# A graph network on one core: statistics of the first norm by row tile, convolution tiles from the eighth count step, attention in steps of five, and ScalarE empties what VectorE emptied

## The reference, cut to what matters

```
h  = relu(layernorm(x))
xn = batchnorm(h)                                   # needs mean and variance over all 1250 rows
conv = relu(segment_mean(xn[src], dst) @ W_conv + b_conv)
q, k, v = h[:256] @ Wq, h[:256] @ Wk, h[:256] @ Wv  # 8 heads of 64
qf = exp(q@proj.T - diag - max)/16 + eps ; kf likewise  # 256 random features
att = (qf @ (kf.T v)) / (qf @ sum(kf)) @ Wo
x  = x + batchnorm(conv + att + h)
h  = relu(layernorm(x)); agg = segment_sum(h[src], dst)
x  = x + h + relu(bn(relu(bn(((1+eps)*h + agg) @ W1 + b1)) @ W2 + b2))   # as in the reference
```

## Time and profile before

| what | us |
|---|---|
| median of three runs | 421.27 |
| the profiled execution, as timed | 421.14 |
| its span, first to last instruction | 419.3 |
| TensorE busy | 384.6 (92%) |
| VectorE busy | 231.5 (55%) |
| ScalarE busy | 166.9 (40%) |
| last first-layer block (A32) handed to VectorE | 232.68 from the span's start |

### The profile page before, as it was taken

How to read it: one execution, slowest core, us unless ns; L and a number is a source line. 1 busy time by engine, 2 the same in 40 slices (tenths; PEclk the granted TensorE clock), 3 DMA queues, 4 the chain that set the end, 5 groups by cost and what they waited for, 6 DMA issues and landing times.

```text
span 419.3 us, 5944 instructions
## 1 busy us (share of the span) xinstructions
PE 384.6 (92%) x1987; PEld 279.5 (67%) x1987; DVE 231.5 (55%) x587; ACT 166.9 (40%) x292; POOL 94.2 (22%) x149
## 2 busy tenths in 40 slices
PE   2799998599869988999999998899999999999995
PEld 1587655366435644666655565545899999999992
DVE  5882889864533455572767788841235344441323
ACT  1465337275463545201002576731264445332131
POOL 7030000200000000000002268882146564011100
PEclk9999999799989999999999999999999999999998
DMA  7930203000000000000490002020000003001212
GB/s 201 274 103 4 98 3 100 2 1 2 0 2 0 3 0 2 2 2 0 122 225 2 1 2 100 29 76 2 0 2 2 2 0 100 2 11 51 61 50 73
DMA packets 16577, 17.96 MB, mean 43 GB/s; under 512 B 1813, under 2 KB 10965, under 8 KB 16537
## 3 DMA queue, kind: packets, MB, share of 16 engines
q1 hardware_dynamic: 15779, 17.28, 14.9%
q10 hardware_dynamic: 758, 0.16, 0.2%
HBM read 14.88 MB, written 2.56 MB: 42 GB/s over the span
## 4 chain that ended last, share of the span: by engine, by line
PE 64%; DVE 14%; issue 9%; ACT 7%; POOL 3%; DVEq 2%; DMA 0%; SPq 0%; POOLq 0%; ACTq 0%
PE bank L1162 62%; DVE ring L831 3%; DVE st_f L904 1%; ACT hn L610 1%; DVE hl L1050 1%; POOL ln_s L427 1%; PE bank L1183 1%; DVE w_lo L1069 1%; POOL x L465 1%; DVEq L831 1%; ACT qf L582 1%; DVE st_row L1061 1%; PE bank L1514 1%; DVE x L1058 1%; DVEq L937 1%
## 5 line engine op out<-in xcount | busy, mean ns | idle before, releaser
L1162 PE MATMUL bank<-AT,hh 125*128 125x400 f16 (+1 forms) x240 | 80.9, 339 | 2.6 <-DVE hl L1050 2.6
L1162 PE MATMUL bank<-AT,hl 125*128 125x400 f16 (+1 forms) x240 | 80.7, 338 | 0.0
L831 DVE TENSOR_SCALAR ring<-iota_code,code 125x500 f16<-125x500 f16 x200 | 54.0, 345 | 0.0
L436 POOL TENSOR_TENSOR bn_tmp<-var_eps,minus_half 128x1 f32<-128x1 f32 (+1 forms) x15 | 9.6, 642 | 189.3 <-DVE var_eps L910 189.2
L826 DVE TENSOR_TENSOR S<-iota_lane,slo 125x1024 f16<-125x1024 f16 x25 | 18.7, 750 | 57.0 <-PE bank L1162 52.3
L1162 PE MATMUL bank<-ring,S 125*128 125x500 f16 x200 | 48.5, 386 | 0.0
L1162 PE MATMUL bank<-wB,hn 128*125 128x512 f32 x80 | 38.4, 625 | 5.6 <-ACT hl L520 5.5
L1162 PEld LDWEIGHTS bank<-ring,S 125*128 125x128 f16 x200 | 28.5, 145 | 19.0 <-issue 8.3
L1162 PEld LDWEIGHTS bank<-AT,hh 125*128 125x128 f16 x240 | 23.2, 97 | 21.6 <-DVE hl L1050 3.3
L1162 PEld LDWEIGHTS bank<-AT,hl 125*128 125x128 f16 x240 | 23.3, 97 | 18.3 <-issue 0.2
L1162 PE MATMUL bank<-a_hi,w_hi 128*128 128x400 f32 (+1 forms) x96 | 34.2, 356 | 0.0
(11 more groups left out here) (190 smaller groups left out, 677.3 us busy)
## 6 DMA issues: line engine op xcount, KB each, us to landing
x_in<-x SPq DMA_DIRECT2D x5, 448.0 KB
x<-x SPq DMA_DIRECT2D x2, 1120.0 KB
w_s<-w SPq DMA_DIRECT2D x2, 1024.0 KB, 9.6
w_s<-w SPq DMA_DIRECT2D x4, 512.0 KB, 3.8
out<-x SPq DMA_DIRECT2D x8, 224.0 KB
wB<-wk SPq DMA_DIRECT2D x1, 1024.0 KB, 8.3
wA<-wq SPq DMA_DIRECT2D x1, 1024.0 KB, 12.6
wB<-wv SPq DMA_DIRECT2D x1, 1024.0 KB, 5.1
```

The lines of the kernel that those rows point to most:

```text
L436: own.step(pool.tensor_tensor(bn_tmp[:, 1, k:k + n], var_eps[:, k:k + n], minus_half[:, 0:n], ALU.pow))
L831: ins = dve.tensor_scalar(ring[:, slot, j, :], iota_code[0:CH], code[:, bass.ds(c + j, 1)], float(-CODES * t), ALU.subtract, ALU.is_equal)
L1162: return pe.matmul(o, l, r, start=start, stop=stop, skip_group_check=True)
```

## The change

The pieces move to other steps. The counts, the products and the transposes are the same instructions in the same number.

1. W_conv gets its own place (`wC`) and is loaded behind the tiles of x at the start, and not into `wB` after V1. Its sum of squares is taken by ScalarE in step 2 (`SQ_AT`), `FR` moves to step 4 and into bank 7.
2. The first norm's statistics are taken per row tile: 40 `bn_stats` of 125 columns, four for each tile in the VectorE step after the tile's transposes; the end of them is in step 5.
3. G0 moves from step 12 to step 8. V1 moves from step 7 to step 6. The attention's pieces of one head pair now repeat every five steps.
4. ScalarE's order in a step: pieces that wait for VectorE (`UQ`, `MX`) come last among the pieces; `hn` of tile i+2 comes after the AT copy of the step, and not before it.
5. `D0`, `D1` and the seven A blocks inside the steps are copied out of PSUM by ScalarE (`rdb`, and `raw` with two buffers), and VectorE works on the copies. Their statistics are taken after WO1, together.
6. `SPAN` becomes one more product in `P`. `O0` moves to bank 6; A00 to A30, A01 and A21 are in bank 7.
7. The load of x for the residual waits for WO1 alone.

```diff
 SLOTS = [s.split() for s in (
-    "hT0 hT1 hT2 K0 K1", "hT3 hT4 PT Q0", "hT5 hT6 N1 Q1", "hT7 hT8 N0 UK0", "hT9 P UQ0", "V0", "MX0", "V1 QT0",
-    "KV0 UK1 SPAN", "SQ UQ1", "FR O0 MX1", "QT1 H", "KV1 UK2 G0", "R0 O1 UQ2 G1", "R1 G2", "R2 MX2 QT2 G3",
...
+    "hT0 hT1 hT2 K0 K1", "hT3 hT4 PT Q0", "hT5 hT6 N1 Q1", "hT7 hT8 N0 UK0", "hT9 FR P UQ0", "V0", "MX0 V1", "QT0",
+    "KV0 UK1 G0", "R0 O0 UQ1 G1", "R1 G2", "R2 MX1 G3", "R3 QT1 G4", "R4 KV1 UK2 G5", "R5 O1 UQ2 G6", "R6 G7",
+    "R7 MX2 G8", "R8 QT2 G9", "R9 KV2 UK3 D0", "O2 UQ3 A00", "A10", "MX3 A20", "QT3 A30", "KV3 D1 A01",
+    "O3 A11", "TA0 TA1 A21 WO0 WO1")]
+SQ_AT, H_AT = 2, 7
...
-LAST = "A01 A11 A21 A31 D2 A02 A12 A22 A32".split()
+LAST = "A31 D2 A02 A12 A22 A32".split()
...
             def conv_high(i):
                 ps = read_group(act, f"G{i}")
                 copy(hh[:, i, :], ps[0:L, :]).then_inc(sem("s_gh"), 1)
-                if i + 2 < T:
-                    normed(i + 2)
...
+            def counts_out(name):
+                c = int(name[-1])
+                c0, w = COLS[c]
+                ps = read_group(act, name)
+                if name[0] == "D":
+                    free_group(copy(rdb[:, c0:c0 + w], ps[:, 0:w]), name)
+                else:
+                    n = RAW.index(name)
+                    if n >= 2:
+                        act.wait_ge(sem("s_raw"), n - 1)
+                    free_group(copy(raw[:, n % 2, 0:w], ps[:, 0:w]), name)
...
             for t in range(len(SLOTS)):
-                for name in SLOTS[t] if t else ():
+                for name in sorted(SLOTS[t], key=lambda name: name[:2] in ("UQ", "MX")) if t else ():
...
                 if t < NW:
                     act.wait_ge(sem("s_win"), t + 1)
                     copy(AT[:, :, t * W:(t + 1) * W],
                          banks[t % 2][0:L, 0:CODES].rearrange("p (a b) -> p a b", a=T)).then_inc(sem("s_at"), 1)
+                if t == H_AT:
+                    normed(0)
+                    normed(1)
+                for name in SLOTS[t]:
+                    if name[0] == "G" and int(name[1]) + 2 < T:
+                        normed(int(name[1]) + 2)
...
+            def tile_stats(i):
+                dve.wait_ge(free[PLACE[f"hT{i}"][0]], PLACE[f"hT{i}"][1] + 1)
+                for f in range(FB):
+                    own.mark(dve.bn_stats(st_1[:, f, i, :], hT[:, f, i * L:(i + 1) * L]))
```

More of the change, by code:

```diff
@@ L83 @@
 LONE_BANKS = {name: bank for bank, names in enumerate((
[L84 to L87, removed]
+    "", "", "K0 N1 D1 TA0", "K1 A11 TA1", "PT Q1 WO0", "Q0 N0 WO1",
+    "hT0 hT2 hT4 hT6 hT8 P MX0 MX1 MX2 MX3 KV0 KV1 KV2 KV3 O0 O1 O2 O3",
+    "hT1 hT3 hT5 hT7 hT9 FR V0 V1 D0 A00 A10 A20 A30 A01 A21 " + " ".join(f"G{i}" for i in range(T))))
+    for name in names.split()}
+LAST_BANKS = (6, 0, 1, 2, 3, 7)
 assert len(LAST_BANKS) == len(LAST)
@@ L137 @@
 W1_AT = (3, 7)
+RAW = [name for slot in SLOTS for name in slot if name[0] == "A"]
 OUT_TILES = [(0, 4), (4, 8), (8, 10)]
@@ L193, in gnn_kernel @@
         cgb = place("cgb", [P, 2, FB], F32, 7.90625)
-        sqr = place("sqr", [P, FB, D], F32, 92)
+        sqr = place("sqr", [P, FB, D], F32, 100)
         head_sel = place("head_sel", [P, FB, HEADS], F32, 7.75)
@@ L268, in gnn_kernel @@
         hn = place("hn", [P, 2, FB, L], F32, 88)
+        wC = place("wC", [P, FB, D], F32, 92)
+        raw = place("raw", [P, 2, COLS[0][1]], F32, 100)
+        st_1 = place("st_1", [P, FB, T, 6], F32, 108)
         tmpr = place("tmpr", [P, 2, COLS[0][1]], F32, 109.1875)
@@ L657, in _ @@
                         rows(i)
+                if t == SQ_AT:
+                    conv_weights()
                 if t < NW:
@@ L883, in attention @@
                     c0, w = COLS[int(name[1])]
-                    ps = read_group(dve, name)
                     dve.wait_ge(sem("s_bn1"), 1)
-                    own.step(dve.tensor_scalar(rdb[:, c0:c0 + w], ps[:, 0:w], 1.0, wscale[:, 0:1], ALU.max, ALU.mult))
-                    n_deg[0] = own.mark(dve.reciprocal(rdb[:, c0:c0 + w], rdb[:, c0:c0 + w]))
-                    dve.sem_inc(free[PLACE[name][0]], 1)
+                    d = rdb[:, c0:c0 + w]
+                    if name in LAST:
+                        ps = read_group(dve, name)[:, 0:w]
+                    else:
+                        dve.wait_ge(free[PLACE[name][0]], PLACE[name][1] + 1)
+                        ps = d
+                    own.step(dve.tensor_scalar(d, ps, 1.0, wscale[:, 0:1], ALU.max, ALU.mult))
+                    n_deg[0] = own.mark(dve.reciprocal(d, d))
+                    if name in LAST:
+                        dve.sem_inc(free[PLACE[name][0]], 1)
                 elif name[:2] == "WO":
@@ L958, in further_chunks @@
                 dve.end_ifs()
-            units = [0]
+            units, held, att_in = [0], [], [False]
             def mean_rows(name):
@@ L989, in piece @@
                 if name == "WO1":
+                    att_in[0] = True
                     own.after(own.n)
-                    for f in range(FB):
-                        own.mark(feature_stats(f, 0, hT[:, f, 0:COLS[0][1]]))
+                    for early in RAW:
+                        f, ci = int(early[1]), int(early[2])
+                        if early in held:
+                            own.mark(feature_stats(f, ci, hT[:, f, COLS[ci][0]:sum(COLS[ci])]))
             load_range(0)
@@ L1011, in _ @@
                         row_stats(i)
[L1012 to L1026, removed]
+                for name in SLOTS[t - 1] if t else ():
+                    if name[:2] == "hT":
+                        tile_stats(int(name[2]))
+                        if name == f"hT{T - 1}":
+                            own.after(own.n)
+                            for f in range(FB):
+                                own.mark(dve.bn_aggr(mv_f[:, f, :], st_1[:, f].rearrange("p c s -> p (c s)")))
+                            own.after(own.n)
+                            feature_terms(0, FB).then_inc(sem("s_mv1"), 1)
                 for name in SLOTS[t]:
@@ L1218, in attention @@
             def attention(name):
[L1219 to L1224, removed]
                 if name == "FR":
```

50 lines of the change are left out of this document (25 added, 25 removed), and 2 rows, old and new, of the table SLOTS.

## The result

The changed kernel took 429.94 us as the median of its runs (428.41 to 433.42), the kernel before 421.28 us beside it (421.06 to 421.43): a ratio of 1.0218 with an interval of 1.0156 to 1.0279. It is slower, as forecast, but by 8.7 us and not by the 2.5 of the sum, and its time lies above the range. The profiled execution took 429.83 us with a span of 428.0.

A forecast was written before the change was run, and what follows sets the result against it. TensorE was taken as the bound, losing 20.4 us to waits and slow clock; new losses 3.55 + 16.55 + 2.6 + 0.2 = 22.9 gave +2.5 on 421.14, 423.6 us; range 421.0 to 426.2, with rivals 419.0 to 427.2.

The forecast's parts named there:

- What bounds the kernel, and what is removed: TensorE's waits for ScalarE and the slow clock cost the kernel before 20.4 us between 60 and 163 us.
- The convolution term: Steps 10, 11, 12, 15, 16, 17: TensorE waits for the late hl copy, 16.55 us in all, bounds 11.5 to 18.5.
- Statistics and the early steps: Steps 4 to 8: FR, KV0 and G0 start late, 3.55 us in all; a tile's statistic costs 0.20.
- The clock: Behind three waits of over 3 us ahead of G: one and a half falls, 2.6 us; none 0, all 5.1.
- VectorE is late: Rival, chance 0.12: early tile statistics at 0.28 each add 1.6 us at KV0; with three clock falls, 427.7 us.
- the order pays: Rival, chance 0.24: clock stays at 1.00 behind all waits, KV0 and G0 wait for nothing; 17.6 us lost, 418.4 us.
- Tail, evictions, loads: No waits from step 18; the last blocks lose 0.2 us, or 1; ScalarE's block copies and the loads cost 0.

The follow-up runs named there:

- e1: The changed kernel with the four hn instructions put back directly behind the hh copy, ahead of the exps and the AT copy; 425.74 us.
- e3: The changed kernel with ScalarE's whole old order: exps where the list has them, hn behind hh, ahead of the AT copy; 417.03 us.
- e9: The changed kernel with TensorE's seven long waits filled with unused products, those ahead of KV0 in bank 7; 424.77 us.
- e6: The changed kernel with tile 9's statistics and the moments put behind MX0's piece in step 6; 426.49 us.
- e2: The changed kernel with the exps of UQ and MX back in their list place, ahead of the hh copy; 427.38 us.
- e5: The changed kernel with ScalarE's order in each step made AT copy, next step's hl copy, hn, then exps; 412.71 us.
- e8: The changed kernel without ScalarE's copies of D0, D1 and the seven early A blocks; VectorE reads the banks; 430.69 us.
- e7: The changed kernel with ScalarE's order of e5 and the late moments of e6; 408.70 us.
- e10: The kernel before with only ScalarE's order changed, to that of e5; 413.25 us.
- e4: The changed kernel with unused products in TensorE's seven long waits, all in the bank of the step's counts; 427.45 us.

## Why the prediction was right or wrong

*What bounds the kernel, and what is removed: right.* The 20.4 us of before between 60 and 163 were the stake: from step 18 to A32 TensorE waits for nothing in the changed kernel, and the second layer takes 186.0 us in both.

*The convolution term: right.* 16.55 was worked out for six waits; they measure 16.45 from start to start (15.6 idle: 3.31, 2.11, 3.14, 3.31, 2.11, 1.63). The places are the ones named, steps 10, 11, 12, 15, 16 and 17. e1 moves the term to the 13.2 that the queue's sums give; e3 moves it to 6.2, where I had put some 8 us. Its lower bound was added up wrongly: the five numbers in the bracket make 11.9 and not 11.5.

*Statistics and the early steps: right in kind, short by some 0.3.* A tile's statistic costs 0.20 as taken, 0.15 and 0.53 being the bounds. Step 4's S came a microsecond later than worked out (49.85 for 48.8), and from step 5's S to step 6's VectorE took 6.02 us (56.82 to 62.84) where 5.0 had been put down; 1.28 of it are the aggregations. So `nbk` came at 66.09 for 64.5, and KV0 waited 2.42 for 1.75. From `nbk` to KV0 the prediction's own 2.67 would have given 67.2 and not 67.45; it measured 3.2. G0's own wait for `hn`, 0.9, didn't come, since KV0 at the low clock was later than `hn`; in e1 and e9, at the full clock, it was 0.39. Early idle time is 3.45, some 3.9 from start to start, against 3.55. e6 shows that tile 9's statistics and the moments held `nbk` back.

*The clock: the step that failed.* I took "one and a half, 2.6" falls, all behind the waits of over 3 us, with three falls, 5.1, as the end. Four came, 8.4 us. The 5.8 that are missing are three things: of the three long waits two had a fall behind them, 3.4 for 2.6, which is 0.8; the waits of 2.30 at G3 and G8 had been given no chance at all, and one of them had a fall, 1.7; and the wait of 1.75 at KV0 had been given none either, came as 2.42, and its fall cost 3.3 where every fall had been priced at 1.7. So the size for the long waits was nearly right, and what failed is that the shorter waits were put at nothing and that a fall behind KV0 was taken to cost what one costs in a G. The evidence for nothing was thin: the pair with 2.13 in it had fallen in the trace before, and 1.84 that didn't was one row.

The runs give a count instead, over the profiled executions of before, after, e1, e2, e3, e5, e6 and e8. Waits of 3.1 to 3.3 ahead of a G: the clock fell behind 11 of 12. Waits of 2.1 ahead of a G, behind a step's normal work: 6 of 8; of 2.55: 1 of 2. Waits of 2.4 to 2.8 ahead of KV0: 5 of 6. Waits of 0.89 to 1.84 ahead of a G: none of 16, and none of 5 more in e7 and e10. Short waits ahead of a KV are another matter: behind 1.27 (e10) and 0.97 (e7) the clock fell, behind 1.75 (before) and 0.98 (e10) it didn't. With the shares ahead of a G the five waits of over 2 us that I forecast would have had 3 x 0.9 + 2 x 0.75 = 4.2 falls, 7.1 us, and the forecast would have been 428.2; with 0.8 of a fall at KV0, at 3.3, it would have been 430.8. The measured 429.94 lies between the two, but the count was made from the same kernel among others, and so this is no test of it.

*Bounds and range.* The rival "VectorE is late", 427.7, had three falls and the larger early wait in it and came nearest, but its price per statistic was wrong: one statistic does take 0.28 as a row, yet the next starts 0.20 after it. It was near by its falls of the clock, and its own 427.7 lay above the end of the stated range. The range ended at 427.2, because each of its cases capped the clock at 5.1. The cap wasn't a bound: the seven waits, six ahead of a G and one ahead of KV0, could each bring a fall, which is 11.9 at 1.7 each, and more with KV0's price.

*Tail, evictions, loads: right at nothing.* VectorE had 0.96 us left ahead of A32's row, and e8 shows no price for emptying the blocks. The last 0.5 us are start-up, for which the prediction had no term.

The other rival, that the order pays, is refuted as it stands, but its first half was true: the 7.6 us of before's long wait and its slow clock are gone. That e3 came near its 418.4 with 417.03 is chance: the rival kept all the waits of the new order and let no fall follow them, while e3 has 6.2 us of these waits and one fall.

## What to carry to other kernels

Read each in-order queue from the side of its neighbour: the copy that gives back a bank TensorE wants next belongs ahead of everything whose reader comes a step later, and 13 us here hung on where four rows of 0.4 us and some exps stood. In this kernel the clock fell behind 23 of the 28 waits of 2.1 to 3.3 us that are counted above, so a wait on TensorE of that length is to be priced with the clock's loss behind it, as an addition of its own for every such wait, and the upper bound is the number of waits and not of the longest ones. A shorter wait isn't safe either, as 1.27 and 0.97 ahead of KV0 show. When one wait is mended, the falls of the clock may only move to the next, as e6 shows, so that the gain of one mended wait may come in part only. The best kernel here, e7, has none above 1.04 in the attention and convolution steps.

## What the runs showed of the hardware

The same wait in the same place can be followed by a low clock in one kernel and not in the next: 2.11 ahead of G3 gave 3.67 in the changed kernel and 5.37 in e2, e6 and e8; 2.42 ahead of KV0 gave 3.06 in the changed kernel and 1.97 in e1. It goes with the spread of the runs: 408.46 at 0.998 beside 412.63 to 413.12 at 0.991 for e5. In e7 the clock fell behind a wait of 0.97, with 0.57 granted from 70 to 72 us, and in e10 behind one of 1.27, with 0.50 from 68 to 70 us. What decides between them these traces don't tell. A fall in a row of G costs 1.7 us nearly each time, with 6.70 and 6.71 (3.0 us) in two rows of e1 and e6; behind KV0 it cost 1.7 (e2, e7), 3.3 (changed kernel, e5, e8) and 4.7 (e3). The row of 32 products at the start took between 8.71 and 10.17 us in kernels that are the same up to there: from 18 to 20 us six products ran in the changed kernel, from 22 to 24 ten, though the profile has a granted clock of 1.00 for both stretches. And TensorE can stop for 2.0 to 2.1 us with no wait to be seen, as in e4 and e9.
